# Local attention inside a whole transformer: another order of TensorE's, ScalarE's and VectorE's work within a tile

## The chip, the cores and the metric

The kernel runs on one core of a Trainium2 chip. The metric is device time in microseconds (us) of one launch of the whole program, from host-laid inputs to output.

## What is computed

The reference is a chain of eight blocks on an input of 8 x 256 x 128 float32. Two of the eight are the same block with the same weights, `ffn`, a six-layer transformer of its own; the change lies in it alone. Cut to what matters:

```
for i in range(6):
    x = attn_layer(shift_tokens(x), Wqkv[i], q_scale[i], k_scale[i], Wo[i]) + x
    x = ffn_layer(shift_tokens(x), ln_g[i], ln_b[i], W1[i], b1[i], W2[i], b2[i]) + x

attn_layer:  q, k, v = split(x @ Wqkv)              # 16 heads of 64
             q = rotary(l2norm(q) * q_scale); k = rotary(l2norm(k) * k_scale)
             out = softmax(8 q k^T, own and previous window of 32) v
             return out @ Wo
ffn_layer:   xn = layernorm(x); a, gate = split(xn @ W1 + b1)
             return a * gelu(gate) @ W2 + b2
```

## The kernel before

The program is written out by hand, engine by engine, with semaphores between them; nothing is scheduled by a planner. Within one `ffn` call the layers follow each other as `body`s: each body is 2 of the 8 sequences, that is 4 tiles of 128 tokens. There are 2 calls x 6 layers x 4 bodies = 48 bodies. In each call the first body stands alone (it has no feed-forward work yet, `feed` is False), five iterations of a hardware loop hold four bodies each, and the last three bodies are written out after it.

A body has four steps, `tt` = 0 to 3 (tiles). This text calls them **step 0 to step 3**. The work is pipelined over tiles: in step `tt` the kernel finishes the attention of tile `tt`, turns (transposes) queries and keys of tile `tt + 1` and makes its scores, and projects tile `tt + 3` to q, k and v. The feed-forward part of the previous body is spread over the steps: layernorm in step 0, the gate half of W1 in step 1, the value half in step 2, W2 in step 3.

What each engine does in a step, with names and lines of the profile:

- **TensorE**: `turn_qk` c = 0 to 3 (lines 419, 421, 422: four transposes for a quarter of queries, or eight for a quarter of keys); `qkv` c = 0 to 5 (line 402: one 128 x 512 block each, 0 to 3 are q and k, 4 and 5 are v); `turn_probs` (line 447); `scores` (line 434, 64 small products for either half of heads); `heads` (line 461, 128 small products in all); in steps 1 and 3 `project` half 0 and half 1 (line 477). Of the feed-forward part `mean` and `variance` (lines 486, 490), `gate` (497), `value` (501), `down` (510).
- **ScalarE**: `exps` (789), `copy_turned` (784), `copy_qkv` (759 and 760: a copy and a square of each of blocks 0 to 3; 762: the copy of blocks 4 and 5), `shift` (824, 825), `write_mask` (794), `copy_probs` (801), `rnorm` (773, 775), `copy_heads` (809), `copy_projected` (817), `enter` (745, 746), `square_centred` (831), `inverse_deviation` (835, 837), `copy_gate` (841), `gelu` (846, 847, between two table loads).
- **VectorE**: `softmax_norm` (948, 950, 954), `norms` (959, 961), `softmax_shift` (940, 943), `add_rotated` (976), `unit_length` (970), `add_stream` (981); of the feed-forward part `centre` (987), `normalise` (993, 996), `gated` (1002), `add_down` (1008).
- **GpSimd** rotates what `unit_length` leaves (1085, 1088). **SyncE** and ScalarE's queue issue DMAs. Neither's order is touched, but for the places of three weight loads on ScalarE's queue.

All block results (`qkv`, `mean`, `gate`, `value`, `down`) share two PSUM banks, 0 and 1. A block can be computed only when its bank's last block was read; TensorE's waits for this are the calls `chunk_read`, `mean_read`, `var_read`, `gate_read`, `value_read`, `down_read` ahead of each block. Transposed quarters share two other banks, and a turn waits for the copy of the turn before the last. `project` half 0 waits for the first of the two copies of `copy_heads`, half 1 for the second:

```python
if half == 0:
    if b == 0 and uu == 0:
        pe.wait_ge(wo_loaded, (run + 1) * LOADS_WO)
    pe.wait_ge(o_copied, nth(g, HEAD_PER, n))
else:
    pe.wait_ge(o_copied, nth(g, HEAD_PER, n - 1) + 2)
```

Every engine takes its instructions in the order written. So the order of the work is the text of the three functions `body` in `fa_tensor`, `fa_scalar` and `fa_vector`.

## Time and profile before

| | |
|---|---|
| time of three runs | 6244.44, 6261.02, 6260.62 us (median 6260.62) |
| the profiled execution | 6260.15 us, of it 6258.4 us span |
| TensorE, ScalarE, VectorE, GpSimd busy | 77%, 69%, 65%, 41% |
| mean granted TensorE clock | 0.857 |
| the two `ffn` calls | about 850 to 2760 us and 3600 to 5480 us of the span |

The page's second part (the span in 40 slices) shows the two calls as the stretches in which GpSimd and the DMA queues work. Within them TensorE is busy in nine tenths of each slice; outside them the program is unchanged.

### The profile page before, as it was taken

How to read it: one execution, taken by the hardware profiler on the slowest of the kernel's cores; microseconds unless marked ns; L12 is line 12 of the kernel's file. 1: busy time of each engine (PE TensorE's matmuls, PEld its weight loads, DVE VectorE, ACT ScalarE, POOL GpSimd, SP SyncE). 2: the span in 40 equal slices, each digit the busy share in tenths (PEclk: the TensorE clock that was granted, in tenths of full speed). 3: DMA queues.
4: the chain of work that ended last, by engine and by line, in shares of the span. 5: the costliest groups of instructions: out<-in, count | busy, mean ns of one | idle time of the engine just before them, and what ended most of it. 6: DMA issues, size and time to landing. Idle time of an engine off the chain costs nothing. (4 is left out here: it accounts for less than half of the span.)

```text
span 6258.4 us, 173182 instructions
## 1 busy us (share of the span) xinstructions
PE 4807.1 (77%) x67664; PEld 3029.3 (48%) x67664; DVE 4095.6 (65%) x6192; ACT 4296.0 (69%) x8831; POOL 2539.7 (41%) x1027
## 2 busy tenths in 40 slices
PE   1000049999999999987777789999999999868779
PEld 0000026666666666653333356666666666634444
DVE  5555567677777776746555567677677777656876
ACT  4333337777777777756999867777777777658668
POOL 0000035556555555622444366555655556400000
PEclk6555569999999999987666689999999999979889
DMA  1000012222222222210000022222222222100000
GB/s 50 0 0 0 0 51 55 66 58 66 57 67 59 64 59 65 61 41 1 1 0 0 18 50 64 62 63 63 64 60 66 62 64 60 47 9 3 0 3 8
DMA packets 181346, 248.30 MB, mean 40 GB/s; under 512 B 52076, under 2 KB 80232, under 8 KB 180072
## 3 DMA queue, kind: packets, MB, share of 16 engines
q1 hardware_dynamic: 176264, 221.95, 14.3%
q10 hardware_dynamic: 4320, 15.73, 0.9%
q8 instruction: 534, 8.75, 0.6%
q14 instruction: 228, 1.87, 0.1%
HBM read 43.50 MB, written 5.24 MB: 8 GB/s over the span
## 5 line engine op out<-in xcount | busy, mean ns | idle before, releaser
L402 PE MATMUL PS<-arena 128*128 128x512 f32 x2304 | 1230.8, 620 | 68.1 <-ACT arena L760 37.4
L1085 POOL TENSOR_TENSOR lns<-arena 128x1024 f32<-128x1024 f32 x192 | 560.0, 2917 | 1062.1 <-DVE arena L970 963.6
L1085 POOL TENSOR_TENSOR arena<-arena 128x1024 f32<-128x1024 f32 x192 | 593.7, 3092 | 440.6 <-DVE arena L970 440.6
L959 DVE TENSOR_REDUCE arena<-arena 128x32 f32<-128x2048 f32 x192 | 438.9, 2286 | 411.6 <-ACT arena L760 411.6
L1455 PE MATMUL PS<-arena 128*128 128x512 f32 x8 | 6.4, 971 | 801.5 <-DVE arena L1389 801.5
L461 PEld LDWEIGHTS PS<-arena 64*64 64x64 f32 x24576 | 501.2, 139 | 161.1 <-issue 150.1
L461 PE MATMUL PS<-arena 64*64 64x32 f32 x24576 | 529.9, 226 | 31.3 <-issue 30.3
L1088 POOL TENSOR_TENSOR lnc<-arena 128x1024 f32<-128x1024 f32 x192 | 531.7, 2769 | 0.0
L759 ACT ACTIVATE arena<-PS 128x512 f32<-128x512 f32 x768 | 478.7, 623 | 46.0 <-PE PS L402 33.9
L1088 POOL TENSOR_TENSOR arena<-arena 128x1024 f32<-128x1024 f32 x192 | 505.7, 2634 | 0.0
L2412 POOL TENSOR_TENSOR arena<-arena 128x1024 f32<-128x1024 f32 x128 | 298.0, 2358 | 475.1 <-ACT arena L2261 475.1
L784 ACT ACTIVATE arena<-PS 128x512 f32<-128x512 f32 x768 | 479.3, 625 | 12.9 <-PE PS L419 6.8
L760 ACT ACTIVATE arena<-PS 128x512 f32<-128x512 f32 x768 | 484.9, 631 | 0.0
L402 PEld LDWEIGHTS PS<-arena 128*128 128x128 f32 x2304 | 367.9, 194 | 201.7 <-ACT arena L760 68.0
L970 DVE TENSOR_TENSOR arena<-arena 128x1024 f32<-128x1024 f32 x384 | 459.0, 1237 | 9.0 <-ACT arena L775 9.0
L2171 PE MATMUL PS<-arena 32*128 32x512 f32 x768 | 323.3, 964 | 165.7 <-DVE arena L2319 132.8
L434 PE MATMUL PS<-arena 64*32 64x64 f32 x24576 | 384.8, 217 | 64.7 <-issue 49.3
L434 PEld LDWEIGHTS PS<-arena 64*32 64x32 f32 x24576 | 342.3, 105 | 145.9 <-issue 145.9
L809 ACT ACTIVATE arena<-PS 128x512 f32<-128x512 f32 x384 | 207.7, 593 | 274.6 <-PE PS L461 274.6
L1455 PEld LDWEIGHTS PS<-arena 128*128 128x128 f32 x8 | 2.4, 320 | 805.4 <-DVE arena L1389 802.4
L2326 DVE SCALAR_TENSOR_TENSOR arena<-arena,PS 128x1024 f32<-128x1024 f32 x192 | 230.7, 1215 | 243.9 <-ACT arena L2255 243.6
L762 ACT ACTIVATE arena<-PS 128x512 f32<-128x512 f32 x384 | 229.4, 598 | 227.6 <-PE PS L402 223.1
(267 smaller groups left out, 11216.6 us busy)
## 6 DMA issues: line engine op xcount, KB each, us to landing
arena<-arena SPq DMA_DIRECT2D x2880, 64.0 KB, 2.0
arena<-in_L_ffn_Wqkv ACTq DMA_DIRECT2D x30, 512.0 KB, 4.1
arena<-in_L_ffn_Wo SPq DMA_DIRECT2D x48, 128.0 KB, 2.8
scratch<-arena SPq DMA_DIRECT2D x4, 1024.0 KB, 4.9
arena<-scratch SPq DMA_DIRECT2D x4, 1024.0 KB, 8.0
arena<-in_L_ffn_W SPq DMA_DIRECT2D x12, 341.0 KB, 3.0
arena<-in_L_ffn_Wqkv SPq DMA_DIRECT2D x6, 512.0 KB, 4.8
arena<-in_ffn_scales SPq DMA_DIRECT2D x12, 128.0 KB, 3.0
```

Source lines behind the costliest of these rows:

```text
L402: pe.matmul(PS[:, QKV + bank, :], xs[uu % 2][:, par * P:(par + 1) * P], w, start=True, stop=True).then_inc(qkv_ready, 1)
L434: last = pe.matmul(PS[w * WIN:(w + 1) * WIN, SCORE + s, m * FD:(m + 1) * FD], qT[s * FD:(s + 1) * FD, m, w * WIN:(w + 1) * WIN], KT[uu % 2 ...
L461: last = pe.matmul(PS[(m % 2) * FD:(m % 2 + 1) * FD, HEAD + head_index(tt, s) % 2, at:at + WIN], VW[par][rows, w, m * FD:(m + 1) * FD], PT ...
L759: act.activation(chunk(raws[tt % 2], c), PS[:, QKV + bank, :], ACT.Copy)
L760: act.activation(chunk(sq, c), PS[:, QKV + bank, :], ACT.Square).then_inc(qkv_copied, 1)
L784: act.activation(to, PS[:, TURN + n % 2, :].rearrange("p (m t) -> p m t", m=4), ACT.Copy)\
L959: dve.tensor_reduce(nrm[:, 3, :], h3(sq), AX_X, ALU.add).then_inc(norm2_own, 1)
L970: dve.tensor_tensor(h3(raw[:, part]), h3(raw[:, part]), rn, ALU.mult).then_inc(u_ready, 1)
L1085: pool.tensor_tensor(halves(heads(t2)), halves(heads(raws[par]))[:, :, ::-1, :], sine, ALU.mult)\
L1088: pool.tensor_tensor(heads(t1), heads(raws[par]), cosine, ALU.mult).then_inc(t1_ready, 1)
L2171: last = pe.matmul(PS[:, 2 * k + s, :], b0_KM[n % 2][rows_of(s), kt * P:(kt + 1) * P], b0_qb[(par + i // CHUNKS) % 2][rows_of(s), :, qt * ...
L2412: pool.tensor_tensor(w3, w3, tri, ALU.mult).then_inc(b0_masked, 1)
```

## The change

Not an instruction is added or removed; they are put in another order, and five blocks in other banks. In the diff, `PROJECTION_BANK` names the bank of each `qkv` block. Its core (of `body` in each engine, the places that the prediction speaks of; the last lines of a call's end change only one wait):

```diff
-        PROJECTION_BANK = ((0, 1, 0, 1, 0, 1), (0, 1, 0, 1, 1, 0), (1, 0, 1, 0, 0, 0), (0, 1, 0, 0, 0, 1))
+        PROJECTION_BANK = ((0, 1, 0, 0, 1, 1), (0, 1, 0, 1, 1, 0), (1, 0, 1, 0, 0, 1), (0, 1, 0, 0, 0, 1))
...
                 turn_qk(g, 1, 0)
+                turn_qk(g, 1, 1)
                 chunk_read(g, 2, 4)
                 qkv(run, b, 3, 0, 0)
-                turn_qk(g, 1, 1)
                 chunk_read(g, 2, 5)
                 qkv(run, b, 3, 1, 1)
                 turn_qk(g, 1, 2)
                 chunk_read(g, 3, 0)
                 qkv(run, b, 3, 2, 0)
                 turn_qk(g, 1, 3)
-                chunk_read(g, 3, 1)
-                qkv(run, b, 3, 3, 1)
                 if feed:
-                    chunk_read(g, 3, 2)
-                    mean(g, 0)
+                    chunk_read(g, 3, 1)
+                    mean(g, 1)
+                chunk_read(g, 3, 2)
+                qkv(run, b, 3, 3, 0)
                 turn_probs(g, 0, final)
                 scores(g, 1, 0)
                 scores(g, 1, 1)
                 if feed:
+                    mean_read(g)
+                else:
+                    chunk_read(g, 3, 1)
+                qkv(run, b, 3, 4, 1)
+                if feed:
                     chunk_read(g, 3, 3)
-                    variance(g, 1)
+                    variance(g, 0)
                 heads(g, 0, 0, final)
                 heads(g, 0, 1, final)
-                if feed:
-                    mean_read(g)
-                else:
-                    chunk_read(g, 3, 2)
-                qkv(run, b, 3, 4, 0)
-                if feed:
-                    var_read(g)
-                else:
-                    chunk_read(g, 3, 3)
+                chunk_read(g, 3, 4)
                 qkv(run, b, 3, 5, 1)
 
                 turn_qk(g, 2, 0)
+                turn_qk(g, 2, 1)
                 if not final:
-                    chunk_read(g, 3, 4)
+                    if feed:
+                        var_read(g)
+                    else:
+                        chunk_read(g, 3, 3)
                     qkv(run, b, 4, 0, 0)
-                turn_qk(g, 2, 1)
...
                 heads(g, 1, 1, final)
+                project(run, b, 0, 0)
+                project(run, b, 0, 1)
                 if not final:
                     if feed:
                         gate_read(g, 1)
                     else:
-                        chunk_read(g, 4, 3)
-                    qkv(run, b, 4, 4, 1)
-                project(run, b, 0, 0)
...
+                if feed:
+                    if final:
+                        gate_read(g, 2)
+                    else:
+                        chunk_read(g, 5, 2)
+                    value(g, 0, 1)
                 turn_probs(g, 2, final)
                 scores(g, 3, 0)
                 scores(g, 3, 1)
+                if not final:
+                    chunk_read(g, 5, 3)
+                    qkv(run, b, 5, 4, 0)
+                heads(g, 2, 0, final)
+                heads(g, 2, 1, final)
+                if feed:
+                    value_read(g, 0)
+                    value(g, 1, 1)
...
-                heads(g, 3, 0, final)
-                heads(g, 3, 1, final)
                 if not final:
                     chunk_read(g, 6, 3)
                     qkv(run, b, 6, 4, 0)
+                heads(g, 3, 0, final)
+                heads(g, 3, 1, final)
                 project(run, b, 1, 0)
+                project(run, b, 1, 1)
                 if not final:
                     if feed:
                         down_read(g, 1)
                     else:
                         chunk_read(g, 6, 1)
                     qkv(run, b, 6, 5, 1)
-                project(run, b, 1, 1)
...
+                    if feed and tt == 0:
+                        shift(g, b)
                     if ahead:
                         copy_turned(g, tt + 1, 1)
-                    if feed and tt == 0:
-                        shift(g, b)
                     if further:
                         copy_qkv(g, tt + 3, 1, PROJECTION_BANK[tt][1], True)
...
-                    if ahead:
-                        copy_turned(g, tt + 1, 2)
                     if further:
                         copy_qkv(g, tt + 3, 2, PROJECTION_BANK[tt][2], True)
                     if ahead:
+                        copy_turned(g, tt + 1, 2)
                         copy_turned(g, tt + 1, 3)
                         write_mask(g, tt + 1)
...
+                    if tt % 2 == 1:
+                        copy_projected(g, tt // 2)
                     if further:
                         copy_qkv(g, tt + 3, 5, PROJECTION_BANK[tt][5], True)
                     if reload and tt == 0:
                         load_projection(l, 2)
-                    if tt % 2 == 1:
-                        copy_projected(g, tt // 2)
...
-                    if feed and tt == 2:
-                        gated(g, 0, 1)
                     if ahead:
                         softmax_shift(g, tt + 1)
                     if feed and tt == 3:
                         add_down(g, b, 1, 1)
                     if feed and tt == 2:
-                        gated(g, 1, 1)
-                    if feed and tt == 0:
-                        normalise(run, b, 1)
+                        gated(g, 0, 1)
                     if nearer:
                         add_rotated(g, tt + 2)
                     if feed and tt == 2:
-                        gated(g, 2, 1)
+                        gated(g, 1, 1)
+                        gated(g, 2, 0)
+                    if feed and tt == 0:
+                        normalise(run, b, 0)
                     if further:
                         unit_length(g, tt + 3)
```

On ScalarE the copy of block 4 and, in even steps, `enter` now stand ahead of `rnorm` and `copy_heads`; they stood behind both.

The order on TensorE at the end of step 3, from `turn_probs` on (L461 is `heads`, L402 a `qkv` block, L477 `project`, L510 `down`). Before:

```order
L447 MATMUL PS<-ident,arena 128x128 x8
L434 MATMUL PS<-arena 32x64 x32
L391 ISA
L510 MATMUL PS<-arena 128x256 x3
L434 MATMUL PS<-arena 32x64 x32
L454 REGISTER_ALU
L246 REGISTER_ALU
L461 MATMUL PS<-arena 64x32 x64
L376 REGISTER_ALU
L402 MATMUL PS<-arena 128x512
L473 REGISTER_ALU
L477 MATMUL PS<-arena 128x256 x4
```

and now:

```order
L510 MATMUL PS<-arena 128x256 x3
L434 MATMUL PS<-arena 32x64 x32
L376 REGISTER_ALU
L402 MATMUL PS<-arena 128x512
L454 REGISTER_ALU
L246 REGISTER_ALU
L461 MATMUL PS<-arena 64x32 x64
L473 REGISTER_ALU
L477 MATMUL PS<-arena 128x256 x4
L475 REGISTER_ALU
L477 MATMUL PS<-arena 128x256 x4
```

Block 4 stood between `heads` and `project`; it now stands ahead of `heads`, and nothing stands between `heads` and `project`.

The order on TensorE in the second half of step 2 (L501 is `value`). Before:

```order
L447 MATMUL PS<-ident,arena 128x128 x8
L434 MATMUL PS<-arena 32x64 x64
L376 REGISTER_ALU
L501 MATMUL PS<-XN,arena 128x512
L454 REGISTER_ALU
L246 ISA
L461 MATMUL PS<-arena 64x32 x64
L376 REGISTER_ALU
L402 MATMUL PS<-arena 128x512
L501 MATMUL PS<-XN,arena 128x512
L376 REGISTER_ALU
L402 MATMUL PS<-arena 128x512
```

and now:

```order
L501 MATMUL PS<-XN,arena 128x512
L447 MATMUL PS<-ident,arena 128x128 x8
L434 MATMUL PS<-arena 32x64 x64
L376 REGISTER_ALU
L402 MATMUL PS<-arena 128x512
L454 REGISTER_ALU
L246 ISA
L461 MATMUL PS<-arena 64x32 x64
L501 MATMUL PS<-XN,arena 128x512
L376 REGISTER_ALU
L501 MATMUL PS<-XN,arena 85x512
L402 MATMUL PS<-arena 128x512
```

The first `value` block moved ahead of `turn_probs`, block 4 ahead of `heads`, and block 5 behind all three `value` blocks.

## Rows read from the trace of the kernel before

**Rows 1.** Stretches: us, busy PE, PEld, DVE, ACT, POOL, clock, DMA, GB/s.
```profile
986.90:2692.90 1706.00, 1617.32 (x27721) 1111.23 (x27720) 1218.89 (x1100) 1270.56 (x2332) 998.69 (x372) 0.98 0.25 62
3718.60:5408.20 1689.60, 1604.80 (x27721) 1104.82 (x27720) 1213.51 (x1100) 1270.70 (x2332) 1003.13 (x374) 0.99 0.25 62
4795.99:4869.95 73.96, 71.43 (x1261) 49.39 (x1260) 54.64 (x50) 57.65 (x106) 48.37 (x21) 1.00 0.30 77
```
**Rows 2.** TensorE's waits, 900 to 2700 us: total, times, longest.
```profile
PE PS L434 <- issue: 27.7, 20, 2.6
PE PS L461 <- issue: 12.9, 20, 1.3
```
**Rows 3.** The same, 3700 to 5430 us.
```profile
PE PS L461 <- issue: 14.2, 26, 1.1
```
**Rows 4.** TensorE, step 0: start, us, line, operation, shape, count [idle before <-releaser].
```profile
1843.51 0.60 PE L419 MATMUL PS<-ident,lnc 128*128 128x128 f32 x4
...
1849.28 1.13 PE L402 MATMUL PS<-arena 128*128 128x512 f32 x2 [0.40 <-ACT arena L760]
1850.75 1.13 PE L486 MATMUL PS<-XN,mean_w 128*128 128x512 f32 x2 [0.34 <-ACT arena L760]
...
1859.70 1.13 PE L402 MATMUL PS<-arena 128*128 128x512 f32 x2 [0.20 <-DVE XN L996]
1860.83 0.66 PE L419 MATMUL PS<-ident,arena 128*128 128x128 f32 x4
```
**Rows 5.** Timeline of ScalarE in the same step, and the next step's first.
```profile
1843.99 1.05 ACT L789 ACTIVATE arena<-arena 128x1024 f32<-128x1024 f32 x1
...
1852.66 0.59 ACT L760 ACTIVATE arena<-PS 128x512 f32<-128x512 f32 x1
...
1861.51 1.06 ACT L789 ACTIVATE arena<-arena 128x1024 f32<-128x1024 f32 x1
```
**Rows 6.** Timeline of VectorE in the same step.
```profile
1853.28 2.29 DVE L959 TENSOR_REDUCE arena<-arena 128x32 f32<-128x2048 f32 x1 [0.69 <-ACT arena L760]
...
1855.71 1.23 DVE L940 TENSOR_REDUCE arena<-PS 128x16 f32<-128x1024 f32 x1
...
1858.11 0.75 DVE L993 SCALAR_TENSOR_TENSOR PS<-XN,arena,PS 128x512 f32<-128x512 f32 x1
...
1859.56 1.22 DVE L976 TENSOR_TENSOR arena<-arena 128x1024 f32<-128x1024 f32 x1
```
**Rows 7.** Timeline of TensorE, end of step 1: `heads`, block 4, `project`.
```profile
1872.68 2.52 PE L461 MATMUL PS<-arena 64*64 64x32 f32 x128
1875.14 1.12 PE L402 MATMUL PS<-arena 128*128 128x512 f32 x2
1876.10 1.90 PE L477 MATMUL PS<-arena 128*128 128x256 f32 x8
```
**Rows 8.** TensorE, step 1 of the last body of the first call.
```profile
2721.45 2.52 PE L461 MATMUL PS<-arena 64*64 64x32 f32 x128
2724.65 3.73 PE L477 MATMUL PS<-arena 128*128 128x256 f32 x16 [0.68 <-ACT arena L809]
```
**Rows 9.** Timeline of TensorE, then VectorE, in step 2 (1880.43 to 1897.87 us).
```profile
1887.92 1.88 PE L434 MATMUL PS<-arena 64*32 64x64 f32 x128 [0.36 <-ACT PS L794]
1896.05 1.12 PE L402 MATMUL PS<-arena 128*128 128x512 f32 x2 [0.82 <-ACT arena L762]
1897.87 0.60 PE L419 MATMUL PS<-ident,arena 128*128 128x128 f32 x4
1888.81 2.29 DVE L959 TENSOR_REDUCE arena<-arena 128x32 f32<-128x2048 f32 x1 [3.78 <-ACT arena L760]
...
1895.84 0.74 DVE L1002 SCALAR_TENSOR_TENSOR arena<-PS,arena 128x512 f32<-128x512 f32 x1
```
**Rows 10.** Stretches around a wait for issue, columns as in rows 1.
```profile
1014.00:1016.00 2.00, 0.52 (x24) 0.32 (x17) 1.97 (x2) 0.42 (x1) 2.00 (x2) 1.00 0.00 0
1018.00:1020.00 2.00, 2.00 (x38) 1.18 (x38) 2.00 (x2) 1.03 (x3) 0.00 (x0) 0.50 0.00 0
```

91 lines of the change are left out of this document (42 added, 49 removed).

## The prediction

> **What bounds the kernel now.** I read the span in slices first, then the stretches of the two calls, then one body. In the calls TensorE is busy 1617 of 1706 us and 1605 of 1690 us at a granted clock of 0.98 and 0.99; ScalarE 1271, VectorE 1219, GpSimd 999 in the first [rows 1]. So TensorE's in-order program sets the time, and an edit is worth what it does to TensorE's waits. Each stretch holds 22 bodies: 77.5 us each in the first, 76.8 in the second, against 73.96 for a body that nothing disturbs [rows 1]. There are two kinds of loss. The undisturbed body has its own small waits on ScalarE and VectorE. The 3.6 and 2.8 us on top hold the waits "for issue" inside the small products of `scores` and `heads`: 40.6 us in the first call, and in `heads` alone 14.2 in the second [rows 2, 3]. After one of them, with TensorE idle most of 2 us at a granted clock of 1.00 (2.4 GHz), the clock is 0.50 (1.2 GHz) four us later [rows 10].
>
> The undisturbed body divides into 17.32 us (step 0: 1843.51 to 1860.83 [rows 4]), 19.6 (step 1, to about 1880.4), 17.44 (step 2, to 1897.87 [rows 9]), and 19.6, which is what 73.96 leaves for step 3. In it the waits are 0.40, 0.34 and 0.20 us in step 0 [rows 4] and 0.36 and 0.82 in step 2 [rows 9]. Steps 1 and 3 have none. I walk each step with the trace's distances from start to start.
>
> **Steps 1 and 3: a new wait ahead of `project`.** `heads` takes 2.46 us (1872.68 to 1875.14). Block 4 behind it takes 0.96, and `project` starts at 1876.10 without a wait, since ScalarE's first `copy_heads` ran under block 4 [rows 7]. The change takes block 4 away from there. What is then left is seen in the last body of a call, which has no block 4: `heads` at 2721.45, `project` at 2724.65, 3.20 us for 2.46 us of work, with 0.68 shown idle for ScalarE's L809 [rows 8]. So the wait costs 3.20 - 2.46 = 0.74 us, twice a body. `project` half 1 waits for the second copy, which ends under half 0. Steps 1 and 3 become 20.35 us each: **+1.5 us a body**.
>
> **The start of every step.** Block 5's copy now follows `copy_projected` on ScalarE. In the old step 0 block 5 stood last, at 1859.70, and the next `exps` began at 1861.51, 1.81 us later [rows 4, 5]. A block that doesn't wait takes 0.96 [rows 7], so `exps` will begin about 0.85 us into each step. Before, in steps 0 and 2, it was 0.48 (1843.51 to 1843.99) [rows 4, 5]. I take 0.8: ScalarE's chain of copies is 0.3 us later there.
>
> **Step 0.** `shift` now stands ahead of the copy of turn 1, so turn 3 waits for that copy, and `mean` a little for the square of block 1: by ScalarE's distances some 0.9 us together, in place of the 0.40 and 0.34 (0.74) and what they hold up. `turn_probs` and `scores` start within 0.2 us of where they did. Behind them block 4, `variance`, `heads` and block 5 have nothing to wait for, since `centre`, `square_centred` and the copies are done. The old 0.20 for `normalise`, and the next turn's short wait for `add_rotated` behind it, go. What decides the end is VectorE. Block 3's square began at 9.15 us into the step [rows 4, 5]; I put it at 9.35. Then +0.62 to `norms`, +2.43 to `softmax_shift`, +2.40 through it, +1.2 for `add_rotated` and +1.5 for `normalise` (0.75 twice) [rows 5, 6]: 17.5. TensorE needs it (`var_read`) at block 0 of step 1, two turns of queries (0.87 us) into that step. So step 0 counts as 16.65: **-0.7**. `unit_length` then keeps VectorE 2 us into step 1, but `turn_probs` there has moved behind `gate` 0, so I let it find its input in time.
>
> **Step 2.** The waits of 0.36 (mask) and 0.82 (block 4's copy, behind gelu and its table loads on ScalarE) go: `value` 0 covers the first, and block 5 now comes last. In their place `value` 1 waits for `gated` 0, which stands behind `softmax_shift` now. `norms` began 8.38 us into the step (1888.81 - 1880.43) [rows 9]. New: `norms` at 8.7 (0.3 later), `softmax_shift` at 11.1, `gated` 0 at 13.5, and done 0.75 later [rows 6, 9] at 14.3. TensorE is through `heads` at about 13.3 (its 12.8 of old less the mask's 0.36 and plus a block of 0.96): a wait of 1.0 us. Then 0.96 each for `value` 1, `value` 2 and block 5: 17.2, **-0.25**.
>
> **Sum.** +1.5 - 0.7 - 0.25 = +0.55 us a body, times 48 bodies: +26 us. Against it stands the wait for issue in `heads`: 12.9 + 14.2 = 27.1 us over both calls [rows 2, 3]. In steps 0 and 3 one block more now stands between `scores` and `heads`, the two runs of small products. The least that this gives is nothing, since the instructions are as many; the most is all 27.1. I take 12: two of four steps, and nearly the whole of a wait there. The waits in `scores` (27.7 us in the first call [rows 2]) I leave, for what precedes them hardly moves. Net +14 us: 6260.15 + 14 = 6274 us for the profiled execution, which is 0.5 us from the median of the three runs, so the same number serves for both.
>
> The Trainium skill (Runtime: NRT & Kernel Launch, "Instruction fetch mechanics") says that instructions stream in sequentially, in blocks, hidden behind their dispatch, and that a taken branch is what exposes a fetch. By that rule the credit of 12 us would be nil and the sum 6286 us. The trace speaks against it: 20 + 26 waits for issue inside `heads` in the two calls [rows 2, 3], while their loops branch back only four times each.
>
> **Rivals.**
> *Faster: the relief is larger.* The new pauses ahead of `project` and the spread-out small products give issue time to catch up. Body time above the undisturbed one is 22 x (3.6 + 2.8) = 141 us, of which at least 40.6 + 14.2 = 55 are waits for issue, and part of the rest is half clock behind them. If 0.4 of the 141 goes, that is -56 + 26: 6230 us. For it: bodies without these waits do occur [rows 1]. Against it: the waits in `scores` come late in runs of small products that are as long as before. Chance 0.24.
> *Slower: the clock.* The new waits of 0.7 to 1.0 us stand behind small products, and the clock does fall after a pause among them [rows 10]. The place is `project` in steps 1 and 3. One half-clock stretch of 4 us costs 2 us; this decides, that is outweighs the noise, once a tenth of the 96 new pauses set one off. At one in four it is 24 x 2 = 48 us: 6322 us. Against it: the pause before L434 in rows 10 was near 2 us, and the longest new one is half of that. Chance 0.12.
> The Trainium skill (TensorE: Matmul & The Clock Gate, "A second HAM failure mode: psum-queue depth-cycling") tells that short pauses between groups, often enough, bring the clock down by themselves; by it this rival would be the likely one, and the time 6322 us.
> *Slower: ScalarE and VectorE drift.* The start of every step is 0.3 us later on ScalarE, and VectorE runs without a gap from `norms` in step 0 to `softmax_norm` in step 1. Where one VectorE instruction is stretched by 1 us there, `turn_probs` waits it out. +1 us a body is 48 us: 6322 us. Chance 0.14.
> *The wait is hidden:* if `project`'s new wait did not come, 1.5 x 48 = 72 us would go: 6202 us. Rows 8 show the same neighbours waiting, so 0.03.
>
> **The numbers.** The forecast, +14 us with an error of some 20 from the walk, has 0.47. 0.3% of this kernel, about what its measurement can tell from no change, is 19 us: 6241 to 6279. The forecast gives 0.28 within, 0.15 slower, 0.04 faster; the first rival 0.18 faster, 0.06 within; the clock and the drift 0.20 slower, 0.06 within; the last 0.03 faster. Sum: faster 0.25, same 0.40, slower 0.35. The range reaches from the first rival to the two slower ones, 6228 to 6322 us.
>
> **What would show it.** In the changed profile: L477 idle before for the copy of `copy_heads`, some 0.68 us, about 90 times; the second `value` waiting for `gated` about 1 us in step 2; turn 3 waiting for the copy of turn 1 in step 0; no block waiting for the copy of block 4; an undisturbed body of 74.5 us. The forecast is wrong if such a body is under 74 or over 75.3 us, if the mean clock in the calls leaves 0.98 to 0.99, or if waits for issue in `heads` do not fall below 20 us in sum.

## The result, and the profile after

| | before | after |
|---|---|---|
| median of the comparison | 6261.0 us (10 runs, 6233.98 to 6273.71) | 6222.26 us (10 runs, 6207.01 to 6231.36) |
| ratio, 95% interval | | 0.9939 (0.9923 to 0.9954) |
| profiled execution, its span | 6260.15, 6258.4 us | 6207.01, 6205.2 us |
| mean granted TensorE clock | 0.857 | 0.865 |
| shares of TensorE, ScalarE, VectorE, GpSimd | 77, 69, 65, 41% | 77, 69, 68, 41% |

The change makes the kernel 0.6% faster, 39 us. The forecast was 6274 us with 6228 to 6322 as its range: the time lies on the other side of before, 6 us below the range's lower end. The two profiled executions lie 53 us apart, since the one of after is the fastest of its ten. In the four comparisons of the experiments, the kernel before has medians of 6251.8 to 6254.0 us (67 executions); against those, the gain would be some 30 us. The direction is the same.

First the stretches that answer to [rows 1]: 22 bodies of either call and one undisturbed body of the changed kernel (us, busy PE, PEld, DVE, ACT, POOL, clock, DMA, GB/s).

```profile
981.08:2674.80 1693.72, 1604.69 (x27721) 1112.49 (x27720) 1279.52 (x1101) 1270.04 (x2332) 1000.81 (x373) 0.99 0.25 62
3683.37:5358.30 1674.93, 1592.66 (x27721) 1105.61 (x27720) 1288.59 (x1101) 1270.08 (x2332) 1003.52 (x373) 1.00 0.25 63
1828.39:1903.67 75.28, 72.08 (x1261) 49.94 (x1260) 59.10 (x51) 57.76 (x106) 45.58 (x17) 1.00 0.26 66
```

VectorE is busier, 65% to 68%, by two kinds of instruction that take longer though they are as many: in the first stretch the multiplication of `softmax_norm` (L954, now L959) 2.24 us for 1.90, and the small one of `norms` (L961, now L966) 0.95 for 0.52. Why, no run shows.

22 bodies take 12.3 and 14.7 us less than before. A mean body is 76.99 and 76.13 us, where it was 77.54 and 76.80. But an undisturbed one has become longer: 75.28 us here against 73.96. So the gain is not in the steps as I walked them, but in what disturbs them. By steps (from the first turn of one to that of the next, mean of 22 bodies, first call / second call):

| step | before | after | difference |
|---|---|---|---|
| 0 | 18.79 / 18.97 | 17.09 / 16.91 | -1.70 / -2.06 |
| 1 | 20.58 / 20.31 | 21.77 / 21.31 | +1.19 / +1.00 |
| 2 | 18.26 / 17.49 | 17.51 / 17.18 | -0.75 / -0.31 |
| 3 | 19.92 / 20.04 | 20.63 / 20.73 | +0.71 / +0.69 |

The rest of the 53 us lies in the calls' first and last bodies and tails. The first fed body (one with feed-forward work) starts 5.9 us earlier, the first call's end (last bodies and what follows) gives 13 more, and the second call's start and end 7. I have not walked those parts.

TensorE's waits for issue answer to [rows 2, 3]: total, times, longest. Before, in the second call (3600 to 5400 us):

```profile
PE PS L434 <- issue: 19.3, 15, 2.2
PE PS L461 <- issue: 15.4, 27, 1.1
```

After, first in 900 to 2700 us (with the new waits of that call), then in 3600 to 5400 us:

```profile
PE PS L477 <- ACT arena L815: 31.3, 46, 0.8
PE PS L421 <- ACT arena L790: 22.3, 27, 2.6
PE PS L434 <- issue: 16.6, 13, 2.4
PE PS L501 <- DVE arena L1007: 11.6, 19, 0.9
PE PS L461 <- issue: 2.1, 7, 0.4
```
```profile
PE PS L434 <- issue: 7.0, 7, 2.0
PE PS L461 <- issue: 1.7, 5, 0.6
```

In `heads` they fall from 28.3 us to 3.8, and in `scores` from 47.0 to 23.6: 75.3 us in both calls together become 27.4. Behind such waits the clock falls [rows 10], and that loss shrinks too. I cut the calls into stretches of 20 us, for this sum alone, and added up (1 - granted clock) x 20 over 1000 to 2640 and 3740 to 5340 us (162 rows): 52.4 us before, 22.8 after. The clock of the whole stretches says the same, 0.98 and 0.99 before [rows 1], 0.99 and 1.00 now. This is the **relief**: 48 us of waits and 30 us of half clock (1.2 GHz), 78 us. The bodies give the same figure another way: above undisturbed ones (73.96 us before, 75.14 now) the 44 bodies lost 141 us and lose 62 now, 79 less.

Sorted by step, the waits for issue fell most in `scores` of step 0, from 30.0 to 6.2 us over both calls. `heads` of step 3 follows (10.9 to 0.4), then `heads` of step 0 (8.2 to 1.4) and of step 2 (7.9 to 2.0). Step 1 has as many as before (11.1 and 11.4 us).

The waits of L421 are of two kinds: 0.44 to 0.52 us in an undisturbed body, and 1.8 to 2.7 us in the first body of each further iteration of the hardware loop, four times a call. There ScalarE stands "for issue" ahead of its first `exps`, 2.6 to 3.1 us now and 2.5 to 3.5 us before. The change doesn't touch these.

Now the steps, in the undisturbed body. TensorE at the end of step 0 and the start of step 1 answers to [rows 4]; start, us, line, shape, count [idle before <- releaser]:

```profile
1828.39 1.04 PE L419 MATMUL PS<-ident,lnc 128*128 128x128 f32 x8
...
1833.40 0.33 PE L421 MATMUL PS<-ident,lnc 128*128 128x128 f32 x1 [0.52 <-ACT arena L790]
...
1843.68 1.12 PE L402 MATMUL PS<-arena 128*128 128x512 f32 x2
1844.64 1.04 PE L419 MATMUL PS<-ident,arena 128*128 128x128 f32 x8
1846.02 1.98 PE L402 MATMUL PS<-arena 128*128 128x512 f32 x4 [0.34 <-DVE XN L1001]
```

VectorE in the same step, as in [rows 6]: `norms`, `softmax_shift`, `add_rotated` and the two instructions of `normalise`.

```profile
1838.40 2.29 DVE L964 TENSOR_REDUCE arena<-arena 128x32 f32<-128x2048 f32 x1 [2.16 <-ACT arena L766]
1840.72 0.18 DVE L966 TENSOR_SCALAR arena<-arena 128x32 f32<-128x32 f32 x1
1840.83 1.22 DVE L945 TENSOR_REDUCE arena<-PS 128x16 f32<-128x1024 f32 x1
1842.08 1.22 DVE L948 TENSOR_TENSOR arena<-PS,arena 128x1024 f32<-128x1024 f32 x1
1843.22 1.22 DVE L981 TENSOR_TENSOR arena<-arena 128x1024 f32<-128x1024 f32 x1
1844.36 0.75 DVE L998 SCALAR_TENSOR_TENSOR PS<-XN,arena,PS 128x512 f32<-128x512 f32 x1
1845.14 0.75 DVE L1001 TENSOR_SCALAR XN<-PS,arena 128x512 f32<-128x512 f32 x1
```

`normalise` ends at 1845.89, 17.50 us into the step, which is the 17.5 of the walk. TensorE comes to block 0 after two turns and waits 0.34 us for it. Steps 1, 2 and 3 of TensorE answer to [rows 7, 8] and [rows 9]:

```profile
1856.87 1.46 PE L461 MATMUL PS<-arena 64*64 64x32 f32 x64
1858.25 1.09 PE L497 MATMUL PS<-XN,arena 128*85 128x512 f32 x2
1859.27 1.46 PE L461 MATMUL PS<-arena 64*64 64x32 f32 x64
1861.41 3.73 PE L477 MATMUL PS<-arena 128*128 128x256 f32 x16 [0.68 <-ACT arena L815]
...
1865.84 1.04 PE L419 MATMUL PS<-ident,lnc 128*128 128x128 f32 x8
...
1876.60 2.62 PE L461 MATMUL PS<-arena 64*64 64x32 f32 x128
1880.04 1.98 PE L501 MATMUL PS<-XN,arena 128*128 128x512 f32 x4 [0.82 <-DVE arena L1007]
...
1882.97 1.04 PE L419 MATMUL PS<-ident,arena 128*128 128x128 f32 x8
```
```profile
1894.85 1.12 PE L402 MATMUL PS<-arena 128*128 128x512 f32 x2
1895.91 2.52 PE L461 MATMUL PS<-arena 64*64 64x32 f32 x128
1899.11 3.73 PE L477 MATMUL PS<-arena 128*128 128x256 f32 x16 [0.68 <-ACT arena L815]
```

Every predicted wait is there: `project` idles 0.68 us for the copy of `heads` in steps 1 and 3, and the second `value` idles 0.82 for `gated` in step 2. No wait for the copy of block 4 is left.

### The profile page after: what moved, and what is told of

It is laid out like the page before. It is cut to its first block and busy times, and to the rows that moved or that the text cites. A ratio compares the mean times of both kernels' runs of the same rounds, so it can differ in the third digit from the quotient of the medians.

```text
span 6205.2 us, 173222 instructions
## 1 busy us (share of the span) xinstructions
PE 4764.0 (77%) x67664; PEld 3022.2 (49%) x67664; DVE 4240.0 (68%) x6192; ACT 4294.7 (69%) x8831; POOL 2538.9 (41%) x1027
## 5 line engine op out<-in xcount | busy, mean ns | idle before, releaser
L402 PE MATMUL PS<-arena 128*128 128x512 f32 x2304 | 1198.0, 617 | 30.0 <-ACT arena L766 18.5
L1089 POOL TENSOR_TENSOR lns<-arena 128x1024 f32<-128x1024 f32 x192 | 545.7, 2842 | 1000.7 <-DVE arena L975 724.1
L1459 PE MATMUL PS<-arena 128*128 128x512 f32 x8 | 6.5, 992 | 801.5 <-DVE arena L1393 801.5
L461 PEld LDWEIGHTS PS<-arena 64*64 64x64 f32 x24576 | 493.3, 136 | 196.5 <-issue 195.7
L1092 POOL TENSOR_TENSOR lnc<-arena 128x1024 f32<-128x1024 f32 x192 | 546.4, 2846 | 0.0
L461 PE MATMUL PS<-arena 64*64 64x32 f32 x24576 | 522.7, 223 | 7.4 <-issue 5.9
L402 PEld LDWEIGHTS PS<-arena 128*128 128x128 f32 x2304 | 376.2, 191 | 251.7 <-issue 111.7
L765 ACT ACTIVATE arena<-PS 128x512 f32<-128x512 f32 x768 | 472.9, 616 | 31.4 <-PE PS L402 19.6
L766 ACT ACTIVATE arena<-PS 128x512 f32<-128x512 f32 x768 | 477.9, 622 | 0.0
L975 DVE TENSOR_TENSOR arena<-arena 128x1024 f32<-128x1024 f32 x384 | 459.1, 1237 | 8.2 <-ACT arena L781 8.2
L768 ACT ACTIVATE arena<-PS 128x512 f32<-128x512 f32 x384 | 230.1, 599 | 333.4 <-PE PS L402 332.7
L790 ACT ACTIVATE arena<-PS 128x512 f32<-128x512 f32 x768 | 447.0, 622 | 13.7 <-PE PS L419 6.8
L959 DVE TENSOR_TENSOR arena<-arena 128x1024 f32<-128x1024 f32 x192 | 430.7, 2243 | 21.1
L477 PE MATMUL PS<-arena 128*128 128x256 f32 x1536 | 358.4, 385 | 65.4 <-ACT arena L815 65.4
L434 PE MATMUL PS<-arena 64*32 64x64 f32 x24576 | 380.1, 216 | 31.3 <-issue 23.7
```

Of the source, the lines that this page charges most:

```text
L402: pe.matmul(PS[:, QKV + bank, :], xs[uu % 2][:, par * P:(par + 1) * P], w, start=True, stop=True).then_inc(qkv_ready, 1)
L434: last = pe.matmul(PS[w * WIN:(w + 1) * WIN, SCORE + s, m * FD:(m + 1) * FD], qT[s * FD:(s + 1) * FD, m, w * WIN:(w + 1) * WIN], KT[uu % 2 ...
L461: last = pe.matmul(PS[(m % 2) * FD:(m % 2 + 1) * FD, HEAD + head_index(tt, s) % 2, at:at + WIN], VW[par][rows, w, m * FD:(m + 1) * FD], PT ...
L477: last = pe.matmul(PS[:, HEAD + n % 2, 0:T], Wo[:, m, :], AT[uu][:, m, :], start=(m == 0), stop=(m == PAIRS - 1))
L765: act.activation(chunk(raws[tt % 2], c), PS[:, QKV + bank, :], ACT.Copy)
L766: act.activation(chunk(sq, c), PS[:, QKV + bank, :], ACT.Square).then_inc(qkv_copied, 1)
```

## The experiments

"Issue" is the sum of the waits for issue ahead of L434 and L461 in both calls (those ahead of other lines are left out), "half clock" the sum defined above. Body is the mean of 22 in the first / second call. Times are medians of the comparison; the kernel before had 6253.35 us in the one with e1 to e4, 6251.83 with e5 to e8, 6252.69 with e9 to e12, 6253.99 with e13 to e15.

The last three columns come from one execution each. Three kernels have the same order on all engines but SyncE (before, e2, e7), and their sums are 75.3, 73.9 and 69.6 us of issue and 52.4, 62.8 and 64.0 us of half clock: a difference of 6 us in the one or 12 in the other tells nothing. Some of these executions also lie far from their kernel's median: after 15 us and e3 19 us below, e9 10 us and e14 16 us above.

| run | what it is | us | ratio to before (95%) | body | issue | half clock |
|---|---|---|---|---|---|---|
| before | | 6261.0 | | 77.54 / 76.80 | 75.3 | 52.4 |
| after | | 6222.26 | 0.9939 (0.9923 to 0.9954) | 76.99 / 76.13 | 27.4 | 22.8 |
| e1 | after, `project` covered | 6144.7 | 0.9822 (0.9805 to 0.984) | 75.40 / 74.40 | 30.8 | 19.2 |
| e2 | before, thin window copies | 6254.32 | 1.0 (0.9988 to 1.0012) | 77.45 / 76.68 | 73.9 | 62.8 |
| e3 | before, step 3 spaced | 6234.04 | 0.9971 (0.9959 to 0.9983) | 77.00 / 75.63 | 52.0 | 22.8 |
| e4 | after, `gated` 0 first | 6317.35 | 1.01 (1.0083 to 1.0117) | 78.79 / 78.42 | 35.1 | 53.0 |
| e5 | e1, step 3 unspaced | 6175.6 | 0.9876 (0.9859 to 0.9894) | 76.27 / 75.33 | 62.2 | 44.4 |
| e6 | e1, shift split | 6154.73 | 0.9844 (0.9827 to 0.986) | 75.67 / 74.56 | 37.6 | 22.8 |
| e7 | before, half the window copies | 6253.89 | 1.0005 (0.9994 to 1.0017) | 77.42 / 76.88 | 69.6 | 64.0 |
| e8 | after, turn 1 first | 6222.68 | 0.9955 (0.9941 to 0.9969) | 76.69 / 76.08 | 26.7 | 17.8 |
| e9 | before + step 0 of the change | 6183.91 | 0.9894 (0.9872 to 0.9916) | 76.23 / 75.49 | 62.5 | 35.2 |
| e10 | before + end of step 3 of the change | 6260.97 | 1.0019 (1.0004 to 1.0033) | 77.70 / 76.61 | 53.2 | 31.4 |
| e11 | e1, step 0 unspaced | 6207.97 | 0.9927 (0.9906 to 0.9948) | 76.52 / 76.29 | 32.4 | 17.2 |
| e12 | e1, `scores` halved | 6141.22 | 0.9821 (0.98 to 0.9842) | 74.84 / 74.62 | 14.7 | 4.2 |
| e13 | before + step 1 of the change | 6302.06 | 1.0082 (1.0065 to 1.0099) | 78.27 / 78.01 | 72.5 | 62.8 |
| e14 | before + step 2 of the change | 6225.55 | 0.9953 (0.9937 to 0.997) | 77.20 / 76.66 | 78.2 | 54.6 |
| e15 | e9 + e3 | 6180.18 | 0.9884 (0.9864 to 0.9903) | 76.39 / 75.03 | 47.4 | 26.2 |

**e1: block 5 between `heads` and `project`.** Is the pause ahead of `project` a plain loss, or does it feed the relief? In after, on TensorE in steps 1 and 3, and the copies on ScalarE in the same order (step 1 shown):

```diff
-                project(run, b, 0, 0)
-                project(run, b, 0, 1)
                 if not final:
                     ...
                     qkv(run, b, 4, 5, 0)
+                project(run, b, 0, 0)
+                project(run, b, 0, 1)
```

> The changed kernel with block 5 put between heads and project in steps 1 and 3 (TensorE), and its copy ahead of copy_projected (ScalarE); all else as changed. Theory P (the pause ahead of project is a plain loss of 0.68 us idle, 96 times): the wait of L477 goes from 65 us to under 5, waits for issue in scores and heads stay at some 25 to 30 us over both calls, and the time falls by some 65 to 80 us against the changed kernel: 6145 to 6160 us, ratio to before about 0.982. Rival Q (the pause is what lets instruction fetch catch up, and bought the gain): waits for issue return to 70 us or so with the half-clock stretches behind them, and the time is within 25 us of the changed kernel's, ratio 0.990 to 1.0.

78 us less than after (6222.26 - 6144.7), for 48 x 2 pauses: 0.81 us each. The wait of L477 falls to 1.4 us a call, and issue and half clock stay as low as in after, as theory P had it. The pause was a plain loss.

**e2 and e7: do the window copies slow the supply of instructions?** SyncE copies windows of v beside the runs of small products. e2 copies 16 of 512 columns, so it leaves out 31/32 of v. e7 issues half of the copies and leaves windows 2 and 3 of v out.

```diff
-sp.dma_start(VW[par][rows, w, :], fr[:, s * CH:(s + 1) * CH]).then_inc(vw_ready[par], 16)
+sp.dma_start(VW[par][rows, w, 0:16], fr[:, s * CH:s * CH + 16]).then_inc(vw_ready[par], 16)
```
```diff
-VW_COPIES = (14, 16)
+VW_COPIES = (6, 8)
...
-                for w in range(4):
+                for w in range(2):
```

> The kernel before with each of the copies of v into its windows (2880 DMAs in the page) cut to 16 of 512 columns: as many DMAs, 1/32 of the bytes; the attention's output is computed from mostly zeros, so 31/32 of v is left out. Theory D (instruction fetch loses against these copies for DMA bandwidth, so that TensorE's waits for issue follow them): waits for issue in scores and heads fall from 71 us over both calls to under 20, and the time falls by 80 to 140 us, ratio 0.977 to 0.987. Rival R (fetch is bound by the rate of small instructions, whatever the DMAs do): waits for issue stay at 60 to 80 us and the ratio is within 0.997 to 1.003.

> The kernel before with half of the copies of v into its windows (the windows 2 and 3 of each tile are left out, so half of the attention is computed from other data): 1344 DMAs in place of 2880. After e2 the bytes are ruled out. Theory N (the number of DMAs is what instruction fetch loses against): waits for issue fall by 20 us or more, ratio 0.985 to 0.995. Rival R (fetch is bound by how fast small instructions come one after another): waits for issue stay at 60 to 80 us, ratio 0.997 to 1.003.

Fewer bytes or half as many of these transfers change nothing: the time is that of before, and 73.9 and 69.6 us of waits for issue remain of 75.3.

**e3: the spacing of step 3, by itself and without the pause.** In before, on TensorE alone:

```diff
-                heads(g, 3, 0, final)
-                heads(g, 3, 1, final)
                 if not final:
                     chunk_read(g, 6, 3)
                     qkv(run, b, 6, 4, 0)
-                project(run, b, 1, 0)
+                heads(g, 3, 0, final)
+                heads(g, 3, 1, final)
                 if not final:
                     ...
                     qkv(run, b, 6, 5, 1)
+                project(run, b, 1, 0)
                 project(run, b, 1, 1)
```

> The kernel before with one edit on TensorE alone, at the end of step 3: block 4 ahead of heads, block 5 between heads and project, both halves of project after it. No pause is added. Theory S (a block between scores and heads is what relieves fetch): waits for issue in heads (27 us over both calls) fall by 8 or more and those of step 3 vanish, time 10 to 25 us below before, ratio 0.996 to 0.9985. Rival Q (pauses give the relief): waits for issue as before, ratio within 0.998 to 1.002.

19 us less in the medians, with issue down by 23 us and half clock by 30, though not an instruction is less and the shortest step 3 is even longer (19.81 us for 19.62). The time is in the range of theory S; the place is only in part. `heads` of step 3 waits 0.2 us in place of 10.9, but all `heads` together fall by 6 us (28.3 to 22.1), not by the 8 that were forecast. The larger part is `scores` of step 0, the step behind: 30.0 to 16.3 us. The profiled execution is the fastest of its twelve, so 53 us is more than the typical relief: the 19 us of the medians and the 10 us of the longer step (0.2 x 48) make some 29.

**e4: `gated` 0 ahead of `softmax_shift`** in step 2 of after, as it stood before, to take away the second `value`'s wait:

```diff
+                    if feed and tt == 2:
+                        gated(g, 0, 1)
                     if ahead:
                         softmax_shift(g, tt + 1)
...
-                    if feed and tt == 2:
-                        gated(g, 0, 1)
```

> The changed kernel with one edit on VectorE: in step 2 gated 0 ahead of softmax_shift, where it was before. The waits of TensorE's second value block for VectorE (27.6 us over both calls) should vanish. Theory P: the step is 0.5 to 0.9 us shorter and the time 20 to 40 us below the changed kernel's, ratio to before 0.988 to 0.991. Rival Q: pauses feed the fetch, waits for issue grow by as much, and the ratio stays at 0.9925 to 0.995.

Slower than after by 95 us, which neither theory had. VectorE, 1815 to 1830 us:

```profile
1823.49 0.75 DVE L1007 SCALAR_TENSOR_TENSOR arena<-PS,arena 128x512 f32<-128x512 f32 x1 [1.46 <-ACT arena L853]
...
1828.07 1.60 DVE L1007 SCALAR_TENSOR_TENSOR arena<-PS,arena 128x512 f32<-128x512 f32 x2 [0.31 <-PE PS L501]
```

VectorE stands 1.46 us for gelu. `softmax_shift`, `add_rotated` and the other two `gated` behind it are late by as much, and block 5, which reads the bank of `value` 1, waits for them: in 900 to 2700 us TensorE shows

```profile
PE PS L402 <- DVE arena L1007: 33.2, 17, 2.1
```

The wait of 0.82 us in after is the cheaper of the two. The shortest body is 1.22 us longer than in after (76.33 us for 75.11), 59 us over 48. Most of the rest is clock: half clock is 53.0 us for 22.8. The stretch around one such wait of block 5, which ends at 1036.3 us (columns as in [rows 1]):

```profile
1034.00:1036.00 2.00, 0.26 (x1) 0.00 (x0) 2.00 (x3) 1.38 (x4) 0.00 (x0) 1.00 0.44 108
1037.00:1039.00 2.00, 2.00 (x7) 1.11 (x6) 2.00 (x2) 0.64 (x2) 0.81 (x1) 0.50 0.41 98
```

In the calls of this run TensorE waits 1.5 to 2.1 us for L1007 37 times, and behind 20 of these the granted clock falls to half within 2 us. Behind the pauses of 0.68 us ahead of `project` in after (94 of them) it never does.

**e5: the spacing of step 3 taken back**, in e1: block 4 behind `heads` again, and its copy on ScalarE behind those of `heads`.

```diff
-                if not final:
-                    chunk_read(g, 6, 3)
-                    qkv(run, b, 6, 4, 0)
                 heads(g, 3, 0, final)
                 heads(g, 3, 1, final)
+                if not final:
+                    chunk_read(g, 6, 3)
+                    qkv(run, b, 6, 4, 0)
```

> e1_covered with block 4 of step 3 put back behind heads (TensorE: heads, block 4, block 5, project; ScalarE copies in that order). The reverse of e3, in the new order. Theory S (a block between scores and heads relieves fetch): waits for issue in scores and heads rise from 31 us over both calls to 42 or more, those in heads above all, and the time is 12 to 30 us above e1_covered (6157 to 6175 us). Rival T (the relief comes from the other moves, turns ahead of blocks and gate or value ahead of turn_probs): within 8 us of e1_covered.

31 us slower than e1, at the upper end of theory S, issue and half clock doubled (30.8 to 62.2, 19.2 to 44.4), while the shortest body is the same (72.65 us as the sum of the shortest of each step, 72.79 in e1). So the spacing of step 3 is shown in both directions. Not "in heads above all", though: `heads` of step 3 goes from 0.5 to 11.9 us, and `scores` of step 0 from 5.4 to 28.4.

**e6: `softmax_shift` split**, so that `gated` 0 stands between its maximum and its subtraction, in e1:

```diff
-                        softmax_shift(g, tt + 1)
+                        softmax_shift(g, tt + 1, (lambda: gated(g, 0, 1)) if feed and tt == 2 else None)
...
-                        gated(g, 0, 1)
+                        gated(g, 1, 1)
                     if nearer:
                         add_rotated(g, tt + 2)
                     if feed and tt == 2:
-                        gated(g, 1, 1)
                         gated(g, 2, 0)
```

> e1_covered with VectorE's step 2 in the order: reduce of softmax_shift, gated 0, subtraction of softmax_shift, gated 1, add_rotated, gated 2. The walk says that value 1 no longer waits (29 us of waits of L501 over both calls go) and that the chain behind it, gated 1 before block 5, still comes in time: 0.5 to 0.8 us a body less, time 22 to 38 us below e1_covered, about 6115 us. Rival: as in e4, what is pushed back on VectorE (the subtraction, then exps and add_rotated) is waited for instead, and the time is the same or up to 60 us more.

No gain, as the rival had it. The wait of `value` goes and the shortest step 2 shrinks from 17.09 to 16.43 us, but the shortest step 3 grows from 19.81 to 20.36: block 5 there now waits 0.5 us for `add_down` (L1015), 19 us in both calls. The wait had only moved.

**e8: the copy of turn 1 ahead of `shift`** on ScalarE, in after:

```diff
-                    if feed and tt == 0:
-                        shift(g, b)
                     if ahead:
                         copy_turned(g, tt + 1, 1)
+                    if feed and tt == 0:
+                        shift(g, b)
```

> The changed kernel with one edit on ScalarE: in step 0 the copy of turn 1 ahead of shift, as before the change. TensorE's wait of 0.52 us for that copy (L421 for L790, some 24 us over both calls in undisturbed bodies) should vanish. Theory V (mean waits for the square of block 1, which is as late as before, so the wait only moves there): time within 6 us of the changed kernel's 6222 us, with L486 waiting 0.3 to 0.9 us instead. Rival: the wait was on the path, and 15 to 25 us go.

The wait of L421 for L790 falls from 22.3 and 20.6 us to 8.6 and 9.5 (what is left are the iterations' starts), and the time doesn't move beyond its error (6222.68). Theory V holds: the wait moved to `mean` (L486), 0.7 us at most, which has 26.0 us in both calls. From 900 to 2700 us:

```profile
PE PS L486 <- ACT arena L766: 12.5, 20, 0.7
PE PS L421 <- ACT arena L790: 8.6, 5, 2.6
```

**e9, e10, e13, e14: each step of the change alone**, put into before, with its banks and the reads of them. (In all the change moves eight blocks to the other bank, not five: blocks 3 and 4 of step 0, block 5 of step 2, `mean`, `variance`, the second and third `gate` and the third `value`.) Of e9 (step 0 on all three engines; shortened):

```diff
+                if feed:
+                    mean_read(g)
+                ...
+                qkv(run, b, 3, 4, 1)
                 ...
                 heads(g, 0, 1, final)
-                ...
-                qkv(run, b, 3, 4, 0)
-                if feed:
-                    var_read(g)
-                ...
+                chunk_read(g, 3, 4)
                 qkv(run, b, 3, 5, 1)
...
+                    if nearer:
+                        add_rotated(g, tt + 2)
                     if feed and tt == 0:
-                        normalise(run, b, 1)
-                    if nearer:
-                        add_rotated(g, tt + 2)
+                        normalise(run, b, 0)
```

> The kernel before with the change's step 0 alone (all three engines, its banks, and the wait for the layernorm moved to block 0 of step 1); steps 1 to 3 as before. Spacing theory (a 128 x 512 block between the run of small products of scores and that of heads lowers the waits for issue there and behind them): two parts add up, a body shorter by about 0.7 us as I had walked it (34 us over 48 bodies), and excess over undisturbed bodies lower by some 10 us a call: 50 us faster than before, within 15. Rival (all relief of the change comes from other steps, step 0 brings its walked part only): 25 to 35 us faster, excess as before (81 and 63 us a call).

Of e10 (the end of step 3, and on ScalarE the copy of block 4 ahead of `copy_heads` and `copy_projected` ahead of the copy of block 5):

```diff
+                if not final:
+                    chunk_read(g, 6, 3)
+                    qkv(run, b, 6, 4, 0)
                 heads(g, 3, 0, final)
                 heads(g, 3, 1, final)
-                if not final:
-                    chunk_read(g, 6, 3)
-                    qkv(run, b, 6, 4, 0)
                 project(run, b, 1, 0)
+                project(run, b, 1, 1)
```

> The kernel before with the change's end of step 3 alone: block 4 ahead of heads, both halves of project right behind heads, block 5 behind them, and ScalarE's copies in that order. It differs from the earlier kernel 'before, step 3 spaced' by the uncovered project alone. Additive theory: that kernel's -17 us, plus one uncovered pause a body at 0.8 us (what covering two of them a body gave back), 48 x 0.8 = +39: 15 to 25 us slower than before. Rival (the pause gives the instruction supply time, so that pause and relief offset): within 8 us of before, with an excess well under that of the spaced kernel (64.7 and 32.7 us a call).

Of e13 (step 1 on TensorE and ScalarE; here the end of it on TensorE):

```diff
+                if not final:
+                    chunk_read(g, 4, 3)
+                    qkv(run, b, 4, 4, 1)
...
                 heads(g, 1, 1, final)
+                project(run, b, 0, 0)
+                project(run, b, 0, 1)
...
-                    qkv(run, b, 4, 4, 1)
-                project(run, b, 0, 0)
```

> The kernel before with the change's step 1 alone (gate 0 ahead of turn_probs, block 4 ahead of gate 1, gate 2 between the halves of heads, both halves of project right behind heads). Additive theory: the change is -38 us, step 0 alone -69, step 3 alone +8, so steps 1 and 2 are +23 together; I give step 1 +20 to +45 (48 pauses at 0.8 us are +39, less a little relief, since heads is split and scores were already apart from it). Rival (the pause is paid back by relief here as it was in step 3): within 10 us of before.

Of e14 (step 2 on all three engines; here VectorE):

```diff
-                    if feed and tt == 2:
-                        gated(g, 0, 1)
                     if ahead:
                         softmax_shift(g, tt + 1)
...
-                        gated(g, 1, 1)
+                        gated(g, 0, 1)
                     if nearer:
                         add_rotated(g, tt + 2)
                     if feed and tt == 2:
-                        gated(g, 2, 1)
+                        gated(g, 1, 1)
+                        gated(g, 2, 0)
```

> The kernel before with the change's step 2 alone on all three engines. Walk of the prediction: -0.25 us a body, 12 us; measured undisturbed step 2 of the change is 17.12 against 17.44, 15 us. Additive theory: 5 to 20 us faster than before, undisturbed step 2 of 17.1 to 17.2, excess as before. Rival (two runs of small products stay apart by one block, but value 0 now parts block 3 from turn_probs and relief is larger, as in step 0 or 3): 25 us faster or more, excess down by over 15 us a call.

Against the before of their comparison the medians say: step 0 -69 us, step 1 +48, step 2 -28, step 3 +8. The sum is -41; the product of the four ratios is 0.9947, and the change measured 0.9939 (0.9923 to 0.9954). The four intervals together leave the sum open by some 22 us to either side, so this says that the parts add up roughly, not that they don't act on each other. The forecasts fared badly: step 0 gained more than either theory gave it (at most 65), step 1 lost 3 us more than the most of its range, step 2 has its rival's time without its relief, and step 3 stands at the edge of its rival's 8.

What each is made of, from the table and from the shortest body of the first call (73.93 us before). The sum of the shortest of each step won't do where one step's end is the next one's wait: a step 0 of 16.07 us in e9 is followed by a wait of 0.78 us for `normalise` at block 0 of step 1.

- Step 3: shortest body +1.18 us (75.11), which is +57 over 48 bodies; issue -22, half clock -21. The relief pays for nearly all of the pause.
- Step 0: shortest body -0.40 us (73.53), -19; issue -13 and half clock -17 (its own spacing). Together -49 for -69 measured; the other 20 us are not explained.
- Step 1: shortest body +1.31 us (75.24), +63, and no relief clear of the noise: issue 72.5, half clock 62.8. The mean body says +0.73 and +1.21.
- Step 2: shortest body -0.32 us (73.61), -15, and no relief (issue 78.2). The 28 measured has an interval of about 10 us; the profiled execution, 16 us above its median, is 18 us faster than that of before.

**e15: e9 and e3 together** (both edits as above, in before).

> The kernel before with the change's step 0 and, in step 3 on TensorE, block 4 ahead of heads and block 5 between heads and project. Additive theory: -69 and -18 add up: 80 to 95 us faster than before, 15 to 25 us slower than the covered kernel (-108), which has steps 1 and 2 of the change as well. Rival (the parts share one relief): 65 to 75 us faster, no better than step 0 alone.

74 us less than before, with an interval of 12 us to either side. That is in the rival's range, but the 88 of the sum and the 69 of e9 have errors of their own, so the times don't decide. The traces lean to the rival: 12.8 (e9) and 23.3 (e3) would bring issue from 75.3 to 39, and it is 47.4; 17.2 and 29.6 would bring half clock from 52.4 to 6, and it is 26.2. How far the two share one relief isn't settled.

**e11: block 4 of step 0 back behind `heads`**, in e1, and block 5 in the bank of `variance` (ScalarE's copy of block 4 behind those of `heads`):

```diff
-                ...
-                qkv(run, b, 3, 4, 1)
                 ...
                     variance(g, 0)
                 heads(g, 0, 0, final)
                 heads(g, 0, 1, final)
+                ...
+                qkv(run, b, 3, 4, 1)
-                chunk_read(g, 3, 4)
-                qkv(run, b, 3, 5, 1)
+                if feed:
+                    var_read(g)
+                ...
+                qkv(run, b, 3, 5, 0)
```

> The covered kernel (blocks 5 between heads and project) with block 4 of step 0 put back behind heads, ScalarE's copy with it; only variance stands between scores and heads in step 0. Spacing theory: step 0 counts as step 3 did (+31 us there), less because variance still stands between: 15 to 30 us slower than the covered kernel, all of it in excess and in a wait for normalise of about 0.2 us a body. Rival (only a pair of runs with nothing between them is harmful): within 12 us of the covered kernel.

63 us slower than e1, and not for the reason that either theory named. Issue and half clock are those of e1. Block 5 now waits for `normalise`, which this kernel still has behind `add_rotated`; the row of 900 to 2700 us:

```profile
PE PS L402 <- DVE XN L1003: 25.8, 21, 1.4
PE PS L490 <- ACT XN L837: 10.0, 19, 0.6
```

With 21.4 in the second call the first is 47 us. The second row is `variance`: with block 4 gone from ahead of it, it waits up to 0.6 us for `square_centred`, 20 us in both calls. The two make 67 for the 63 measured. So what e11 shows is what block 4's place covers, and what it is worth that the wait for `normalise` moved to block 0 of step 1: a place two turns later. Whether the spacing of step 0 by itself brings relief it doesn't show; that rests on e9. The 32 waits of 1.0 to 1.4 us for `normalise` brought no fall of the clock within 2 us behind them.

**e12: block 4 between the halves of `scores`** in steps 0 and 1, in e1 (step 1 shown):

```diff
                 scores(g, 2, 0)
-                scores(g, 2, 1)
                 if not final:
                     chunk_read(g, 4, 3)
                     qkv(run, b, 4, 4, 1)
+                scores(g, 2, 1)
```

> The covered kernel with block 4 of steps 0 and 1 between the two halves of scores (64 products each) instead of behind both. Spacing theory: shorter runs of small products wait less, 5 to 25 us faster than the covered kernel, with waits for issue ahead of scores lower than 18.6 and 3.3 us. Rival (scores end 0.96 us later, and VectorE's softmax_shift, which TensorE needs a step later, moves with them; or what counts is the number of small products per step and not how they are cut): the same or up to 20 us slower.

Waits for issue halve once more and the half clock nearly goes. Of e12, 900 to 2700 us:

```profile
PE PS L434 <- issue: 6.5, 10, 1.5
PE PS L461 <- issue: 4.3, 8, 1.0
```

And the time is that of e1 (6141.22 and 6144.7): the waits fell as the first theory had it, and the time did as the rival had it. The shortest step 0 and step 1 are 0.44 us longer each (16.51 for 16.07, 20.27 for 19.83). In a whole body some of that only takes the place of the wait for `normalise` between them, so the shortest body is 0.43 us longer (73.85 for 73.42), 21 us over 48, against 31 us of relief; the rest is within the error. e1 and e12 are the fastest kernels found, 1.8% under before and some 1.2% under the change (0.9822 / 0.9939 = 0.9882).

## Why the prediction was wrong

**The step that failed is the credit for waits for issue.** It read: "The least that this gives is nothing ...; the most is all 27.1. I take 12" and "The waits in `scores` ... I leave, for what precedes them hardly moves." Measured, `heads` gave 24.5 us, `scores` gave 23.4, and the half clock behind both 29.6, which the sum had at nothing: 78 us in place of 12. e3 and e5 show that the spacing of step 3 alone does much of it: 53 and 57 us by the same two sums, 19 and 31 us in the medians. They also show where the reason given was wrong. The waits in `scores` of step 0, the largest of all, do not hang on what directly precedes them but on what stands a step earlier: with block 4 ahead of `heads` or behind it in step 3 they are 5.4 or 28.4 us (e1 and e5). I had bounded the term by one line of the waits instead of by all that such a wait costs. That line left out the clock behind it, though [rows 10] showed it.

**The walk of the body** was right in its mechanisms and too low in sum. Forecast +0.55 us a body, measured +1.2: the medians of the four steps are 16.25, 21.19, 17.13 and 20.57, 75.14 us, for 73.96 (the body of the rows above is one of 75.28).
- Step 0: block 0 of step 1 could start 0.51 us later than two turns allow (1846.02 - 1844.64 - 0.87), so the step counts as 16.76; forecast 16.65. VectorE's chain came out to 0.1 us.
- Steps 1 and 3: the pause was 0.74 to 0.76 from start to start, as forecast. But step 3 took 20.57 for 20.35. e3, which has no pause, shows 0.19 of it (19.81 for 19.62): the blocks' new places cost that by themselves. Step 1, without its 0.51, is 20.68, also for 20.35: `heads` stands there in two halves of 1.38 us, 2.76 in place of 2.46, which the walk left out.
- Step 2: 17.13 for 17.2, with the wait at 0.82 for 1.0.

So +1.2 x 48 = +57 and -78 of relief make -21. The mean bodies say -0.55 and -0.67, or -29 over 48; the rest of the medians' 39 us is within the error and the calls' ends, which no run takes apart. By steps, the forecast -34 us for step 0 (0.7 x 48) met -69, +36 for step 1 met +48, -12 for step 2 met -28, and +36 less the credit of 12 for step 3 met +8.

**The rivals.** "The relief is larger" is what happened: it forecast 6230 us. It named 56 us; with the body as dear as it is, it needed 78. Its other half, that the pauses give issue time to catch up, is refuted: e1 takes the pauses away and keeps the relief. *The clock* fails: 96 pauses of 0.68 us, and the granted clock rose from 0.857 to 0.865; e1, without them, has 0.863. Half clock is 22.8 us with them and 19.2 without. Its mechanism is real for longer pauses: in e4, with 37 waits of 1.5 to 2.1 us, half clock is 53.0 us. The Trainium skill (TensorE: Matmul & The Clock Gate, "A second HAM failure mode: psum-queue depth-cycling") would have had it fall; for pauses of this length and place the trace doesn't agree. *Drift* did not come: the wait of 0.51 us on VectorE at block 0 of step 1 is the one that the walk had. e4 shows what it would cost: one VectorE instruction 1.46 us late made 95 us. *The wait is hidden* fails: 31.3 us a call.

**On the tests named**: L477 was idle 46 times in the first call; the second `value` waited; turn 3 waited for the copy of turn 1. An undisturbed body above 74.5 but under 75.3 us was inside my bound. The waits in `heads` fell to 3.8 us, far below 20, which I had written as the sign of a forecast that holds; it should have had a lower bound too. The clock left 0.98 to 0.99 upward, to 0.99 and 1.00: by this sign the forecast was wrong. That the range was missed by only 6 us is luck: body and relief were both too low, by some 30 us and by 66, and the two errors work against each other.

The Trainium skill's rule on fetch (Runtime: NRT & Kernel Launch, "Instruction fetch mechanics"), by which the order of straight code would leave such waits alone, stands against 75.3 us that became 27.4 by order alone, if these waits are fetches at all, which no run shows. What it says of a taken branch fits the trace: ScalarE's waits of 2.5 to 3.5 us stand where the loop begins anew.

## What to carry to other kernels

Price a wait for issue in a run of many small matmuls with the half clock behind it, and look for long instructions (here one 128 x 512 block of 0.96 us) that can stand between two such runs: moving one block a body took 19 and 31 us off the time here (e3, e5), and over 50 us of waits and clock off the traces. Look for the gain in the runs behind the block too, not only in the next one. When a consumer is moved right behind its producer, as `project` behind `heads`, keep one independent block between them: it cost 0.8 us each time and gave 78 us back. Try each step of a reordering by itself before taking it whole: here one step brought -69 us, another +48. And read a body's length from whole bodies: the shortest of each step, added up, can leave out a wait that passes from one step to the next.

## What the runs showed of the hardware beyond that

- The waits for issue depend on how small products are grouped, not on the window copies: 1/32 of their bytes or half their number left the time at 1.0 and 1.0005 of before, while one moved block a body (e3) took 23 us off these waits, 14 of it in `scores` of the step behind (step 0 of the second call: 18.97 us before, 17.83 in e3).
- With 64 products for 128 between blocks in two steps (e12), both calls lose only 4.2 us to the half clock, against 52.4 before.
- The granted clock fell to half within 2 us behind 20 of 37 waits of 1.5 to 2.1 us (e4), behind none of 32 waits of 1.0 to 1.4 us (e11) and behind none of 94 pauses of 0.68 us (after), each ahead of 128 x 512 or 128 x 256 matmuls.
- Which part of the supply runs short in a run of small products is open: no run measured it.
